# Restacking q and k for causal attention: two stores in half precision parts, one read-back with rows of 4 KB

## What is computed

```python
xn = _layernorm(x, axis=-1)
s = attn(xn, Wqkv, b_qkv, Wout, b_out)
g = _silu(ffn(xn, w_router, w_fc, w_proj))
x = x + s * g
# inside attn:
scores = jnp.einsum('bqhd,bkhd->bhqk', q, k) * scale
scores = scores + bias[None, :, None, :]
scores = jnp.where(causal[None, None, :, :], scores, -1e9)
p = jax.nn.softmax(scores, axis=-1)
ctx = jnp.einsum('bhqk,bkhd->bqhd', p, v).reshape(B, S, D)
return ctx @ Wout.T + b_out
```

## Time and profile before

| | |
|---|---|
| median of 3 runs | 1542.82 us (1542.73 to 1542.98) |
| the profiled execution | 1544.06 us, its span 1542.0 us |
| PE busy | 1416.1 us, 92% of the span |
| DVE, ACT, POOL busy | 936.1, 775.3, 692.2 us |
| mean granted clock of TensorE | 0.976 of full speed |
| all hardware queue transfers | 75808 packets, 105.70 MB, 21.3% of 16 engines' span |

### The profile page before, as it was taken

One profiled execution on the slowest core, in us unless ns is written; L12 is line 12 of the kernel. 1 busy time (PEld: TensorE's weight loads), 2 busy tenths in 40 slices (PEclk: granted clock), 3 DMA queues, 4 the chain that ended last, 5 costly groups with the idle time before them and its releaser, 6 DMA issues. The chain is left out here.

```text
span 1542.0 us, 30070 instructions
## 1 busy us (share of the span) xinstructions
PE 1416.1 (92%) x9912; PEld 897.1 (58%) x9912; DVE 936.1 (61%) x2432; ACT 775.3 (50%) x1826; POOL 692.2 (45%) x900
## 2 busy tenths in 40 slices
PE   2879999999999999998659999999999999999995
PEld 1445565656555555655336666666666666666663
DVE  7577777777777676767449755555444445555542
ACT  3478787777777777787336422222222222222221
POOL 0456557474655656465323433333333333333331
PEclk9999999999999999999869999999999999999998
DMA  4425335343433424333157311111000111111000
GB/s 154 144 76 165 96 104 157 98 145 97 138 104 125 134 92 140 115 106 115 31 178 243 113 42 42 42 42 42 29 28 27 30 42 42 42 42 42 28 15 28
DMA packets 85136, 133.97 MB, mean 87 GB/s; under 512 B 14207, under 2 KB 63359, under 8 KB 82816
## 3 DMA queue, kind: packets, MB, share of 16 engines
q1 hardware_dynamic: 75808, 105.70, 21.3%
q0 software_dynamic: 9184, 26.36, 5.4%
HBM read 98.34 MB, written 34.21 MB: 86 GB/s over the span
## 5 line engine op out<-in xcount | busy, mean ns | idle before, releaser
L1010 PE MATMUL psF<-xT,wf 128*128 128x256 f16 x3264 | 380.7, 274 | 6.7 <-DVE wf L1113 6.7
L1028 PE MATMUL psY<-wf,aT 128*128 x1632 | 374.1, 379 | 0.0
L1010 PEld LDWEIGHTS psF<-xT,wf 128*128 x3264 | 320.4, 98 | 73.9 <-issue 7.4
L1216 POOL TENSOR_TENSOR a<-a 128x512 f32<-128x512 f32 x136 | 157.4, 1157 | 408.1 <-DVE a L1130 406.5
L864 POOL TENSOR_SCALAR pr<-pr,rden 128x128 f32<-128x128 f32 (+3 forms) x512 | 269.0, 544 | 137.2 <-DVE rden L794 135.9
L554 ACT ACTIVATE pr<-pr,mn 128x128 f32<-128x128 f32 (+3 forms) x512 | 281.8, 553 | 0.0
L1028 PEld LDWEIGHTS psY<-wf,aT 128*128 128x128 f16 x1632 | 159.7, 98 | 163.6
L783 DVE CUSTOM_DVE_ANT_0 pr<-psS,base,nsl 128x128 f32<-128x128 f32 (+3 forms) x512 | 250.0, 544 | 2.3 <-PE psS L410 1.9
L431 PE MATMUL psT<-conf,pr 128*128 128x128 f32 x1280 | 207.9, 281 | 23.1 <-POOL pr L864 19.2
L1064 ACT ACTIVATE rl<-psF 128x512 f32<-128x512 f32 x136 | 81.1, 596 | 265.0 <-PE psF L1010 265.0
L337 PE MATMUL psA<-xT,wqkv 128*128 128x512 f16 x768 | 196.7, 395 | 15.5 <-DVE wqkv L636 13.1
(11 more groups left out here) (137 smaller groups left out, 1382.7 us busy)
## 6 DMA issues: line engine op xcount, KB each, us to landing
qk_parts<-pre SPq DMA_DIRECT2D x64, 256.0 KB, 2.2
qs<-qk_parts SPq DMA_DIRECT2D x128, 128.0 KB, 2.6
ks<-qk_parts SPq DMA_DIRECT2D x128, 128.0 KB, 2.6
wst<-in_wf SPq DMA_DIRECT2D x16, 1024.0 KB, 6.3
wstage<-in_wf SPq DMA_DIRECT2D x32, 512.0 KB, 4.6
xin<-in_x SPq DMA_DIRECT2D x32, 256.0 KB, 4.0
attn_out<-so SPq DMA_DIRECT2D x32, 256.0 KB, 2.0
pt<-in_wqkv SPq DMA_DIRECT2D x4, 768.0 KB, 10.3
```

What stands on the lines that cost most here:

```text
L1010: last = nc.tensor.matmul(psF[c % 2][:, k * TT:(k + 1) * TT], w(e, 2 * hc, hl, kc * 512 + col, P), xT[:, r % 2, x, kc, :], start=(m == 0), ...
L1028: last = nc.tensor.matmul(psY[r % 2][h][:], aT[:, c % 4, x, k, h * P:(h + 1) * P], w(e, 2 * hc + 1, hl, q * 512, 512), start=(c == 0 and k ...
L1216: nc.gpsimd.tensor_tensor(at, at, at, ALU.mult).then_inc(s["a_ready"], 1)
```

## The change

Each stack now goes out in two stores, one for each part, and comes back in one read.

- The store of the high part waits for the high part alone (`qk_hi`), and the store of the low part for `qk_lo`. Each moves 128 KB.
- `qk_parts` has another layout in DRAM. Rows are ordered so that what one partition of the stack needs (4 heads x 512 tokens in float16 = 4 KB) lies together: for q by head dimension, then part, then head; for k by part, then head dimension, then head. In `qs` and `ks` the partitions are thereby ordered anew as well, the same way in both.
- The read-back is one transfer of 512 KB into all 128 partitions. q's source is the 64 DRAM rows of 4 KB, named twice by an outermost dimension of 2 with step 0. k's source is the same 64 rows in an outermost dimension of 64, each named twice by an inner dimension.
- The counts of the semaphores are adapted: a stack is 16 instead of 64 on `stacked`, and a pair of stores is 32 instead of 16 on `stored`.

```diff
-                for w, dst, parts in ((0, qs, (0, 1, 0, 1)), (1, ks, (0, 0, 1, 1))):
-                    wait(sp, s["qk_hi"], u * 2 + 1 + w, s["apart_sp"])
-                    wait(sp, s["qk_lo"], u * 2 + 1 + w, s["apart_sp"])
-                    wait(sp, stacked[w][par], (b * 2 + g // 2) * 64, s["apart_sp"])
-                    sp.dma_start(io["qk"][w, par].rearrange("a p n -> p a n"),
-                                 pre[:, w, :, :]).then_inc(stored[w], 16)
-                    wait(sp, stored[w], (u + 1) * 16, s["apart_sp"])
+                for w, dst in ((0, qs), (1, ks)):
+                    order = "(d a j) n -> a j d n" if w == 0 else "(a d j) n -> a j d n"
+                    parts = io["qk"][w, par].rearrange(order, a=2, j=HG, d=HD)
+                    wait(sp, stacked[w][par], (b * 2 + g // 2) * 16, s["apart_sp"])
+                    for a, ready in enumerate((s["qk_hi"], s["qk_lo"])):
+                        wait(sp, ready, u * 2 + 1 + w, s["apart_sp"])
+                        sp.dma_start(parts[a], pre[:, w, a, :]).then_inc(stored[w], 16)
+                    wait(sp, stored[w], (u + 1) * 32, s["apart_sp"])
                     wait(sp, s["S_done"], (u - 1) * 16, s["apart_sp"])
-                    for r in range(4):
-                        sp.dma_start(dst[r * HD:(r + 1) * HD, par, :, :],
-                                     io["qk"][w, par, parts[r]].rearrange("(j d) n -> d j n", j=HG)
-                                     ).then_inc(stacked[w][par], 16)
+                    if w == 0:
+                        src = io["qk"][w, par:par + 1].rearrange("o (m j) n -> o m (j n)", j=HG)
+                        src = src.broadcast_to([2, 2 * HD, HG * S])
+                    else:
+                        src = io["qk"][w, par].rearrange("(m o j) n -> m o (j n)", j=HG, o=1)
+                        src = src.broadcast_to([2 * HD, 2, HG * S])
+                    sp.dma_start(dst[:, par, :, :].rearrange("p j n -> p (j n)"), src).then_inc(stacked[w][par], 16)
...
-                        wait(pe, stacked[w][par], (b * 2 + g // 2 + 1) * 64)
+                        wait(pe, stacked[w][par], (b * 2 + g // 2 + 1) * 16)
...
-                        wait(dve, stored[w], (bj * NG + i) * 16)
+                        wait(dve, stored[w], (bj * NG + i) * 32)
...
-          "qk": nc.dram_tensor("qk_parts", [2, 2, 2, P, S], F16).ap()}
+          "qk": nc.dram_tensor("qk_parts", [2, 2, 2 * P, S], F16).ap()}
```

## The result

The changed kernel took **1694.44 us** (median of 4 runs, 1693.05 to 1697.14) against 1542.78 us before: a ratio of 1.0978, 95% interval 1.0965 to 1.0992. It is 151.7 us slower. The prediction was 1670, range 1595 to 1755, slower with a chance of 0.86. The profiled execution of after took 1693.37 us, its span is 1691.3 us.

A forecast was written before the change was run, and what follows sets the result against it. PE, busy 92% of the span, was taken to bound the kernel. Added PE waits, 8 x 15.7 plus 1.5 = 127 us, on 1544.06 gave 1671, so 1670 for the median; clock and vanishing waits were set against each other; range 1595 to 1755.

The forecast's parts named there:

- The choice of 2 engines: q's read-back, source outer count 2, rides 2 engines at 24 KB/us: 11.0 us moving, 13.2 us to landing; chance 83%.
- The first rival: All 16 engines carry q's read; k of g0 still lands before its scores; 1543 to 1545 us, chance 11%.
- the slow-engine rival: Two engines carry q's read at 15 KB/us each: 17.5 us to move, plus 208 us, about 1880 us; chance 4%.
- The gain of 3 us: Rival: 16 engines, faster 4 KB rows, fewer issues; only the one 2.8 us wait for ks can go; 1540 us, chance 2%.
- The chain: SP's transfers queue in order per engine, k's halves behind q's read; PE waits 15.7 us per pass over units g0 to g3.
- Wait of PE at g0: At unit g0 k's read lands at 231.6, scores wanted it at 221.2: 10.4 us of wait on PE.
- the first unit: g0 of the first pass, with zero room because PE waited there already: pays 11.9 instead of 10.4 us.
- The stall at g2: At unit g2 k lands at 281.3, scores stand at 276.4: PE waits 4.9 us, DVE's wait for stored lies beside it.
- The mis-sized term: Lower PE clock after long waits, up to 27 us, set against vanishing PE waits for DVE and POOL, 33 us.
- The stores: Half stores ride 4 engines: a store ends 0.8 us later if the high half went ahead, 2.3 us behind other work.
- SP's issues: A stack loses two of five issues on SP, some 0.9 us per stack, hidden by the room and bringing nothing.

The follow-up runs named there:

- the kernel with both parts mended: The changed kernel with stores on 16 engines (projection weight columns reordered) and q's stack read back in two transfers of 64 partitions: 1543.6 us, ratio 0.9996.
- the kernel that took 1560 us: The changed kernel with only q's stack read back in two transfers of 64 partitions, source outer count 64: 1560.2 us, ratio 1.0099.

## Why the prediction was right, and where it was off

**The choice of 2 engines** carried the forecast and held: 49 GB/s at a share of 0.13, and 24.5 GB/s per engine against the 24 that were taken between 26 and 21.3. The first rival (16 engines) and the slow-engine rival (15 KB/us) are out by the same rows. The gain of 3 us did not show even in the kernel with both parts mended, which is at 0.9996 of the kernel before.

**The chain.** Time from q's read to k's read in g0: 15.3 us, worked out 15.8. Wait of PE at g0: 8.4 to 10.7 us, mean 9.5 in seven passes, against 10.4; the first unit 15.5 in all, against 2.8 + 11.9 = 14.7. A pass takes 105 us, against 103.

**The stall at g2** was sized too long. The prediction let PE wait 4.9 us at the scores and put DVE's wait for `stored` beside that. In fact DVE waits first, and longer:

```profile
320.93 0.43 DVE L712 CAST pre<-stage 128x512 f16<-128x512 f32 x1 [7.42 <-DMA qk_parts<-pre]
```
```profile
324.99 0.70 PE L414 MATMUL psS<-ks,qs 128*128 128x128 f16 x4 [2.65 <-DMA ks<-qk_parts]
...
430.44 0.70 PE L414 MATMUL psS<-ks,qs 128*128 128x128 f16 x4 [2.74 <-DVE mn L787]
```

It is 7.1 to 7.7 us on DVE and 2.0 to 2.7 at PE's scores, from the second pass on. PE has other work until 322.3, when DVE's wait is over. In three of the eight passes the profile names DVE's step and not k's read as what came last, as in the second row. The two end almost together: in the pass of the first row DVE's step ends at 324.8, and k's read leaves at 320.85 and takes 4.0 us to land in the median. In the first pass DVE's wait was not beside PE's, and PE waited for DVE, a term that the prediction put at nothing:

```profile
111.61 0.43 DVE L712 CAST pre<-stage 128x512 f16<-128x512 f32 x1 [11.41 <-DMA qk_parts<-pre]
```
```profile
112.42 0.69 PE L435 MATMUL psT<-conf,pr 128*128 128x128 f32 x2 [7.80 <-DVE pt L774]
```

PE's waits for the scores' operands came to 104.3 - 2.8 = 101.5 us, or 109.4 with the three of g2 (7.9 us) that are put down to DVE, against 127. The 18 us between are those of g2: 21.0 instead of 39.2 us in eight passes.

**The mis-sized term** is the one where two effects were set against each other. The clock was to cost up to 27 us and the present waits of PE for DVE and POOL, 33 us, to vanish in return. The clock cost what was said, a little more: 32.5 us of additional busy time for the same matmuls. The waits did not vanish. Those for POOL before the transposes (L435) were 19.2 us and are 18.9; those for DVE before the scores were 19.4 and are 16.3, without the three of g2; and the 7.8 us of the first pass came on top. So all idle time of PE rose by 116.8 us, and 116.8 + 32.5 is the 149.3 by which the span grew, where 127 was forecast. The forecast of 1670 is as near to 1694 as it is because two errors have opposite signs: the chain was worked out 18 us too long, and the clock, set to nothing in the sum, cost 32.5. That much of the nearness is luck; the two engines and the wait at g0 are not. The waits for DVE and POOL come within a step, where PE waits for work that depends on PE's last result; that a long stall elsewhere in the pass does not shorten them is read from these numbers.

**The stores** were taken as part of the chain, at 0.8 us more when the high half went ahead and 2.3 us more behind other work. In the kernel with q's read in two transfers, q's read of g1 and of g2 leaves 3.6 and 3.7 us after POOL has ended the low part, before 2.2 us both times: 1.4 and 1.5 us more, not 0.8. Behind `wst`, at g0, it is 2.0 us more, against 2.3. What the prediction did not say is that the stores would cost by themselves. In the rival with 16 engines it had k of g0 stored at 216.6 and landed at 220.2, still 1 us early, and a time of 1543 to 1545. By the rule of its own chain, that k's halves move behind q's read, the sum is 214.6 + 3.1 + 0.7 = 218.4 and the landing 222.0, which is past the scores at 221.2. Measured without the slow read, k's read leaves at 225.26, which is 218.7 in the times of the kernel before, and lands 3.7 us later, at 222.4. With that landing and the stores' share at the first unit (4.9 us, where under 1 was given) the kernel takes 1560 us. Had q's read been carried by 16 engines, the result would by that run have been 1% slower and outside what that rival gave.

**SP's issues** brought nothing, as said, and were priced a little low. A half store takes 0.52 us to issue and a 4 KB read 0.54 to 0.56, against 0.38 and 0.43 before; SP saved 2 x 0.52 + 0.55 = 1.6 against 0.38 + 1.73 = 2.1 us per stack, so 0.5 us went instead of 0.9.

## What to carry to other kernels

Before you merge transfers, write down the outermost count of both sides: a broadcast or a short dimension in front turns 16 engines into 2 or 4, and everything queued behind on those engines lands late with it. Fewer and longer transfers paid nothing here, since the many short ones were hidden with 2.4 us to spare; find the room at the tightest consumer first, then ask who spends it. In a stage where PE sets the time, add the clock to each wait of several microseconds, and do not count on other waits to shrink in return: here some 3 of 33 us did.

## What the runs showed of the hardware beyond that

- With two engines at work and fourteen idle, each moved rows of 4 KB from DRAM at 24.5 GB/s, close to its share of the best stretch with all 16 (26). Two engines are slow because they are two.
- The kernel's time grew in step with the time that q's read moves, 524 KB over the number of engines: 146, 60 and 23 us above the 16-engine case for 2, 4 and 8.
- Issuing cost SP 0.52 us for a store whose DRAM side has an outer count of 4 with 32 rows behind it, 0.38 us for the store of before that carried twice the bytes, and 0.34 us (median) for a half store in the old layout.
- In all the runs the page gives no landing time for a transfer on fewer than 16 engines: `qs` and `qk_parts` in the changed kernel, and both have one again in the kernel where they ride 16. The reverse does not hold. In the kernel that took 1560 us `wst` and `xin` have no landing time either, though these transfers are those of before (why is open), so the missing time alone is no proof; the share of the DMA engines in a short stretch is.
